# A 16-byte bias tensor moved to the end of a stage's SBUF layout

## What is computed

```
x = x + xattn(layernorm(x), ctx, ctx, mask, Wq, bq, Wk, bk, Wv, bv, Wo, bo)
x = x + window_attention(layernorm(x), ...)
x = x + experts_and_shared_ffn(layernorm(x), ...)

def xattn(query, key, value, ...):          # key = value = ctx, (2, 8192, 512)
    q = query @ Wq.T + bq
    k = key @ Wk.T + bk
    v = value @ Wv.T + bv
    att = softmax(heads(q) . heads(k) / sqrt(32))
    return merge(att . heads(v)) @ Wo.T + bo
```

## The kernel before

| tensor | before | after |
|---|---|---|
| WKH, WKL, WVH, WVL (8192 bytes each) | 77632 and on | the same |
| bk_s, bq_s (16 bytes each, so 32 with the step) | 110400, 110432 | 110400, (moved behind kx) |
| bv_s (2048), XN (16384), ln_tmp (480) | from 110464 | from 110432 |
| QH, QL, QQ (4096 each), BLR (512), MI (2048) | from 129376 | from 129344 |
| CH0, CH1, CL0, CL1 (8192 each) | 144224 and on | 144192 and on |
| KH0, KH1, KL0, KL1, VS0, VS1 (8192 each) | 176992 and on | 176960 and on |
| CH0 minus WKH | 66592 = 130 x 512 + 32 | 66560 = 130 x 512 |
| KS0, QS0 (attention) | 59200, 67392: 16 x 512 apart | the same |
| WH0, WH4, XEH0 (experts) | 108768, 190688, 182496: 160 x 512 and 144 x 512 from WH0 | the same |

## Time and profile before

### The profile page before, as it was taken

How to read it: one execution, slowest core, us unless ns; L and a number is a source line. 1 busy time by engine, 2 the same in 40 slices (tenths; PEclk the granted TensorE clock), 3 DMA queues, 4 the chain that set the end, 5 groups by cost and what they waited for, 6 DMA issues and landing times. The chain is left out here.

```text
span 2834.0 us, 37416 instructions
## 1 busy us (share of the span) xinstructions
PE 2799.8 (99%) x14157; PEld 1766.6 (62%) x14157; DVE 2171.7 (77%) x1600; ACT 1722.0 (61%) x2489; POOL 88.0 (3%) x43
## 2 busy tenths in 40 slices
PE   8999999999999999999999999999999999999998
PEld 5888888888744444444444444445554688888886
DVE  5544444444499999999999999946647888888886
ACT  4222111222299999999999999724531477777775
POOL 0000000000000000000000000000000300000000
PEclk9999999999999999999999999999999999999999
DMA  5555555555655555655556565321120699999995
GB/s 217 196 193 178 197 188 178 190 194 178 193 132 139 128 143 126 143 130 140 131 136 143 124 147 122 89 74 46 45 116 30 238 380 348 346 349 345 343 348 197
DMA packets 229104, 515.51 MB, mean 182 GB/s; under 512 B 18130, under 2 KB 84050, under 8 KB 199628
## 3 DMA queue, kind: packets, MB, share of 16 engines
q1 hardware_dynamic: 225372, 505.15, 56.7%
q0 software_dynamic: 3584, 8.39, 1.3%
HBM read 400.03 MB, written 113.44 MB: 181 GB/s over the span
## 5 line engine op out<-in xcount | busy, mean ns | idle before, releaser
L534 DVE TENSOR_TENSOR AC<-AC,PR 128x2048 f32<-128x2048 f32 x448 | 988.6, 2294 | 4.9 <-ACT PR L499 4.9
L499 ACT ACTIVATE PR<-PS 128x512 f32<-128x512 f32 x1024 | 568.7, 612 | 55.2 <-PE PS L421 43.2
L421 PEld LDWEIGHTS PS<-QS,KS 128*128 128x128 f32 x2048 | 365.0, 188 | 336.6 <-ACT PR L503 181.3
L421 PE MATMUL PS<-QS,KS 128*128 128x512 f32 x2048 | 563.6, 416 | 4.6 <-ACT PR L499 3.6
L503 ACT ACTIVATE PR<-PS 128x1024 f32<-128x1024 f32 x512 | 502.9, 1055 | 0.0
L432 PE MATMUL PS<-PR,VC 128*32 128x512 f32 x4096 | 493.0, 599 | 0.7 <-ACT PR L499 0.7
L929 DVE TENSOR_TENSOR WL<-RAW,WH 128x2048 fp32r<-128x2048 f32 x192 | 436.4, 2287 | 58.4 <-ACT WH L924 58.4
L736 ACT ACTIVATE KH<-PS,bk_s 128x512 fp32r<-128x512 f32 x128 | 87.9, 688 | 556.2 <-PE PS L792 556.1
L924 ACT ACTIVATE WH<-RAW 128x2048 fp32r<-128x2048 f32 x192 | 362.0, 1913 | 7.9 <-PE PS L1363 5.2
L631 DVE SCALAR_TENSOR_TENSOR KL<-PS,bk_s,KH 128x512 fp32r<-128x512 f32 x128 | 95.6, 751 | 268.6 <-ACT KH L736 268.6
L432 PEld LDWEIGHTS PS<-PR,VC 128*32 128x32 f32 x4096 | 106.9, 109 | 217.3 <-issue 173.3
(11 more groups left out here) (208 smaller groups left out, 3213.5 us busy)
## 6 DMA issues: line engine op xcount, KB each, us to landing
KS<-kh_d SPq DMA_DIRECT2D x256, 256.0 KB
RAW<-in_gw SPq DMA_DIRECT2D x64, 1024.0 KB, 5.4
RAW<-in_up_w SPq DMA_DIRECT2D x64, 1024.0 KB, 5.1
RAW<-in_down_w SPq DMA_DIRECT2D x64, 1024.0 KB, 5.3
kh_d<-KH SPq DMA_DIRECT2D x32, 1024.0 KB, 4.4
kl_d<-KL SPq DMA_DIRECT2D x32, 1024.0 KB, 6.4
v_d<-VS SPq DMA_DIRECT2D x128, 256.0 KB, 2.9
KS<-kl_d SPq DMA_DIRECT2D x128, 256.0 KB
```

The source lines that it names most:

```text
L421: pe.matmul(PS[:, m % RING, :], KS[N % 2][:, j, t * P:(t + 1) * P], QS[bg % 2][:, j, :], start=True, stop=True).then_inc(s_s, 1)
L499: nc.scalar.activation(PR[tile % BUFS][:, 2 * hp + jj], PS[:, bank + jj, :], ACT.Exp, scale=SCALE).then_inc(s_exp, 1)
L534: v.tensor_tensor(a[i % 2][:], a[i % 2][:], p[:], ALU.add).then_inc(s_acc, 1)
```

## The change

`bq_s`, the bias of the queries, was the second small tensor behind the split weights. It is now made last in the stage, behind `kx`. Everything that lay behind it up to `kx` moves down by 32 bytes, the context halves `CH` and `CL` among it. No instruction is added, removed or moved on any engine: the order of all five is row for row the same, only addresses differ. Tensors of the later stages stay where they were.

```
-            bk_s, bq_s, bv_s = sb("bk_s", [P, G]), sb("bq_s", [P, G]), sb("bv_s", [P, D])
+            bk_s, bv_s = sb("bk_s", [P, G]), sb("bv_s", [P, D])
             XN = sb("XN", [P, TT, D])
             tmp = sb("ln_tmp", [P, TT, 15])
             QH, QL = sb("QH", [P, 2, SQ], F32R), sb("QL", [P, 2, SQ], F32R)
...
             KH = [sb(f"KH{i}", [P, G, CK], F32R) for i in range(2)]
             KL = [sb(f"KL{i}", [P, G, CK], F32R) for i in range(2)]
             VS = [sb(f"VS{i}", [P, KT, D]) for i in range(2)]
-            kx = sb("kx", [P, 4, BG])
+            kx, bq_s = sb("kx", [P, 4, BG]), sb("bq_s", [P, G])
```

## The result

The changed kernel takes 2816.09 us (median of six runs, 2814.52 to 2821.1) against 2837.1 us for the kernel before on the same chips (2833.91 to 2840.53). The ratio is 0.9924 with a 95% interval of 0.9914 to 0.9935. Forecast were 2816.6 us, in a range from 2812 to 2829.

The account below looks back on a forecast made before the run. TensorE was taken to bound the kernel, without gaps in keys and values. 3024 products at 6.67 ns less give 20.2 us, so the 2836.8 us median becomes 2816.6 us, range 2812 to 2829.

Parts of the forecast that it names:

- The bound: Keys-and-values stage: TensorE is busy 694.00 of 694.00 us at the full clock, so its products alone set the length.
- The rate elsewhere as a measure: Keys and values: products would go from 233.3 ns to the experts' settled 226.7 ns, 6.67 ns less each.
- The count: Lines 792 and 800: 3024 products at 6.67 ns less each give 20.2 us, all on the path.
- the bound of 10.0 us: Keys and values: if every group of 12 started disturbed, at 230.0 ns, the gain would be only 10.0 us.
- the sum's own span: Whole kernel: with the seam's and disturbed starts' bounds, the full-effect case at 2816.6 us reaches from 2813 to 2821.
- Other work: Same stage: chunk 0's 48 key products and 64 f32 query products put at nothing, at most 0.7 us; VectorE and ScalarE without effect.
- The seam: From keys and values to attention: moves forward with TensorE's last products; half-clock stretch there kept as 1.7 us uncertainty.
- First scores: Attention start: at about 744.2 us instead of 764.4, then the same 2069.6 us within 2 to the end.
- No effect: Rival: 233.3 ns belongs to the keys-and-values stage, not the 32 bytes; time stays 2836.8 us; chance 0.11.
- Half: Rival: only keys or values get faster, or each group of 12 settles anew; 10.0 us gained, 2826.8 us; chance 0.06.
- Slower: Rival: a multiple of 512 is the worst place, keys and values settle at 236 ns; 2845.0 us; chance 0.06.
- More: Rival: keys and values settle below 226.7 ns, at about 224 ns; 28 us gained, 2808.7 us; chance 0.02.

Follow-up runs that it names:

- experiments 1 to 3: 1: kernel before, CH0 padded by 480 bytes, 2817.85 us; 2: changed kernel, both operands moved 32 bytes, 2817.82 us; 3: changed kernel, WVH/WVL 32 bytes off, 2831.3 us.
- experiments 10: The changed kernel with 448 unused bytes in front of CH0, which is 512 - 64; 2835.4 us in a single run.
- 12: The changed kernel with only WKL and WVL put 32 bytes off, WKH, WVH, CH and CL staying a multiple of 512 apart; 2835.76 us.

## Why the prediction was right

*The bound.* TensorE held the stage alone and still does: 674.00 us busy of 674.00. *The rate elsewhere as a measure.* The step from 233.3 to 226.7 ns was taken from the experts' rows; measured are 226.7 ns, in keys and in values. *The count.* 3024 products at 6.67 ns were to give 20.2 us; 20.0 were measured on the stretch that holds them. Groups of 12 don't start disturbed, so the bound of 10.0 us was rightly not taken. That the time came within 0.5 us of the forecast is partly luck: the six runs of the changed kernel spread over 6.6 us. The low end of the sum's own span, 2813, has no working; the seam's 1.7 us lead to 2814.9. *Other work.* The f32 products of the queries are as they were: from the first start to the last 29.7 us before (25.4 to 55.1) and 29.6 after (26.4 to 56.0). *The seam* moved with TensorE, with the same two waits (0.85 us of TensorE, and ScalarE's for the landing of `v_d`). The clock was counted as an uncertainty of 1.7 us; the 2.1 us gained behind the last values are mostly that, at another place than I named: in the window attention, not at the seam. *First scores* were forecast at 744.2 us and came at 745.28, of which 0.9 us is the later start. From there to the end it took 2067.4 us instead of 2069.6, so that the sign "the same within 2" was missed by a hair, for the same reason.

*The rivals.* "No effect" falls by the result, and that nothing else than the distance made it by experiments 1 to 3, which change the distance and the addresses apart. "Half" falls by the chunk's two equal halves. "Slower", a multiple of 512 as the worst place, falls with them; that the layout 4 bytes off measured 2845.4 us, where 2845.0 had been worked out for this rival, is a coincidence. "More" didn't occur: no kernel settled below 226.7 ns.

*Against the rule of the page.* The page "SBUF — State Buffer" of the Trainium skill (section "Who interferes with whom") lists TensorE's two read ports, for the moving operand and for the weights, as independent and says that TensorE never waits on anyone. Here the measurement differs from what the prediction drew from it, that no address matters: the same reads at a distance 32 bytes off cost 16 cycles per product of 512 columns, in two stages, and the measurement decides. The page "TensorE: Matmul & The Clock Gate" of the Trainium skill (section "Back-to-back issue gap") gives the formula behind the 215.8 ns for a single product by itself, and about 131 ns per product of 512 columns for a stream of weight loads and products; the prediction took the first for a stream. None of the fp32r streams here reaches either; the least that one settles at is 226.7.

What was only argued in the prediction and is now better supported is the cause. That the load of the next weights and the streaming of the moving operand get into each other's way was a reading of two rates; experiments 10 (the sign) and 12 (the place of the delay) are what it rests on now. What inside the array or the memory causes it, why the period is 256 bytes, and why the blocks alternate at 64 and 448 bytes, stays open.

## What to carry to other kernels

Where a stream of fp32r products of 512 columns shows 233 ns from start to start at the full clock instead of 227, look at the addresses of the two operands: put stationary and moving tensors a multiple of 256 bytes apart, which costs a small tensor moved or a few unused bytes. Only products of 128x128 by 512 columns were measured here; for other shapes and types it has to be tried. Read the distance from start to start over some twenty products, since the durations in the profile hide it, and compare it with another stage of the same kernel. One operand of several that is off is enough to lose the whole, and any small tensor put in between later can bring the loss back.

## What the runs showed of the hardware that was not expected

- The relative place of TensorE's two operands costs up to 5% of a dense fp32r stream: 226.7 ns at a distance of 0 or 256 bytes (modulo 512), 233.3 at 32 or 288, 232.6 at 128, and up to 237.8 at 4 (keys).
- The loss is a state of the stream and not a price per product: after slow products some seven fast ones are needed until 226.7 ns are back (241, 224, 231, 236, 228, 232, 231, then 226 and 227), and with one displaced product in three the whole stream is at 233.3.
- VectorE and ScalarE showed nothing of the kind: the subtraction of the halves takes 2281 ns in the kernel before and 2282 at 4 bytes off. Nor did the plain f32 products of the queries (29.7 us before and 29.6 after), of which only these two distances were seen.
